# Convolution from high and low parts, and a new order of the last attention turns

## The reference

```
x = x + 0.5 * moe(LN(x))
x = x + attention(LN(x))
x = x + 0.5 * moe(LN(x))

moe(h):       probs = softmax(h @ router.T)            # 8 experts, the best 2, weights normed
              y = sum_k w_k * (silu(h @ gate_k) * (h @ up_k)) @ down_k     # hidden width 176
attention(h): qkv = causal conv over 3 taps, 256 -> 3 * 64, + conv_b
              blocks of 128 tokens; 8 heads of 64 from q, k, v of width 64, causal softmax
              out = (heads @ wo + bo) @ proj_w + proj_b
```

## Time and profile before

| | |
|---|---|
| median of three runs | 769.83 us |
| profiled execution | 768.44 us, of which span 766.7 |
| PE matmul, busy share of the span | 89% |
| DVE | 68% |
| ACT | 64% |
| POOL | 44% |
| PE on the chain that ended last | 66% |
| q/k convolution (L1529) | 192 records, 46.0 us |
| v convolution (L1538) | 192 records, 24.3 us |
| experts' first product (L1474) | 852 records, 288.7 us |
| DMA, first slice of 40 | 308 GB/s |

### The profile page before, as it was taken

The page is one execution under the profiler, slowest core; times in us unless marked ns, Lnnn a source line. Parts: engine busy times, 40 slices in busy tenths (PEclk is TensorE's granted clock), DMA queues, the critical chain, the costliest instruction groups (busy, mean ns, idle before and its releaser), DMA issues.

```text
span 766.7 us, 19140 instructions
## 1 busy us (share of the span) xinstructions
PE 684.0 (89%) x5321; PEld 587.7 (77%) x5354; DVE 519.3 (68%) x1747; ACT 488.2 (64%) x1735; POOL 336.3 (44%) x361
## 2 busy tenths in 40 slices
PE   4999899999997899999999999999418999999854
PEld 3986799999993677777777777777317999999843
DVE  6578666666664666687878787777654777777653
ACT  4767566666663577777777777767514666666533
POOL 5200544444415544446566665444641445444500
PEclk9999999999998999999999999999757999999968
DMA  9940354544432201112121111100243444444289
GB/s 308 316 136 1 95 150 144 144 132 128 125 100 82 71 28 30 32 32 64 57 66 54 64 57 43 41 32 22 90 112 98 122 133 125 131 124 124 84 302 355
DMA packets 57862, 83.39 MB, mean 109 GB/s; under 512 B 9520, under 2 KB 43827, under 8 KB 57780
## 3 DMA queue, kind: packets, MB, share of 16 engines
q1 hardware_dynamic: 44772, 47.63, 19.9%
q0 software_dynamic: 13008, 34.69, 14.6%
HBM read 45.77 MB, written 37.44 MB: 109 GB/s over the span
## 4 chain that ended last, share of the span: by engine, by line
PE 66%; issue 10%; DVE 8%; POOL 7%; DMA 4%; ACT 3%; SPq 1%; DVEq 0%; POOLq 0%; ACTq 0%
PE CC L1474 18%; PE B L1529 3%; PE CC L1557 3%; POOL yg L666 3%; PE A L1461 3%; PE CC L1615 3%; PE SS L1551 3%; PE F L1605 2%; PE SS L1491 2%; POOL pr L658 2%; PE SS L1492 2%; PE SS L1493 2%; PE F L1625 2%; PE SS L1494 2%; PE SS L1495 2%
## 5 line engine op out<-in xcount | busy, mean ns | idle before, releaser
L630 POOL DMA_INDIRECT shared<-h_rows,tok_i x71 | 66.9, 942 | 116.7 <-DVE tok_i L1071 45.1
L642 POOL DMA_INDIRECT y_rows<-shared,y_dest x71 | 69.8, 984 | 89.1 <-DVE y_dest L1139 75.4
L1474 PE MATMUL CC<-w_hi,rowsT_hi 128*128 x284 | 104.6, 368 | 0.3 <-DVE rowsT_lo L1127 0.2
L658 POOL TENSOR_TENSOR pr<-pr,prec 128x1024 f32<-128x1024 f32 x31 | 58.7, 1893 | 94.9 <-DVE prec L1300 94.9
L1474 PE MATMUL CC<-w_hi,rowsT_lo 128*128 x284 | 92.1, 324 | 0.0
L704 ACT ACTIVATE shared<-CC 128x176 f32<-128x176 f32 x142 | 45.1, 317 | 73.9 <-PE CC L1474 73.9
L1474 PE MATMUL CC<-w_lo,rowsT_hi 128*128 x284 | 92.0, 324 | 0.0
L783 ACT ACTIVATE pr<-SS,nmax 128x128 f32<-128x128 f32 x256 | 90.1, 393 | 1.6 <-DVE nmax L1259 1.6
L1122 DVE TENSOR_TENSOR shared<-shared,CC 128x176 f32<-128x176 f32 x142 | 48.0, 338 | 49.9 <-ACT shared L704 47.6
L675 POOL DMA_INDIRECT h_regions<-h_store,dest x64 | 64.0, 1000 | 38.8 <-DVE dest L1224 21.7
L666 POOL DMA_INDIRECT yg<-y_rows,slot_i x64 | 62.3, 973 | 34.4 <-DMA y_rows<-shared 15.5
(11 more groups left out here) (312 smaller groups left out, 2003.2 us busy)
## 6 DMA issues: line engine op xcount, KB each, us to landing
shared<-h_regions SPq DMA_DIRECT2D x71, 129.0 KB
y_rows<-shared SPq DMA_DIRECT2D x71, 128.0 KB, 1.7
w_lo<-y_rows SPq DMA_DIRECT2D x9, 512.0 KB, 8.0
x_sb<-in_x_dram SPq DMA_DIRECT2D x8, 512.0 KB, 7.7
out_dram<-x_sb SPq DMA_DIRECT2D x16, 256.0 KB, 6.3
w_hi<-y_rows SPq DMA_DIRECT2D x7, 512.0 KB, 11.7
w_lo<-in_gupT_dram SPq DMA_DIRECT2D x2, 1408.0 KB, 12.9
h_regions<-pad_rows SPq DMA_DIRECT2D x15, 129.0 KB, 2.8
```

What stands on the lines that cost most here:

```text
L630: pool.indirect_dma_start(out=rows[:, s % RING, 0:D], out_offset=None, in_=h_dram[:, :], in_offset=bass.IndirectOffsetOnAxis(ap=tok_i[:, s ...
L642: pool.indirect_dma_start(out=y_dram[0:TOPK * TOKENS, :], out_offset=bass.IndirectOffsetOnAxis(ap=y_dest[:, s:s + 1], axis=0), in_=y_sb[:, ...
L658: pool.tensor_tensor(pr[:, q, :, :], pr[:, q, :, :], prec[:, q, :].unsqueeze(2).to_broadcast([P, NH, P]), ALU.mult).then_inc(t["norm"], 1)
L1474: i = pe.matmul(CC[:, 512 * (u % 2):512 * (u % 2) + GU], rows_part[:, u % 2, c * P:(c + 1) * P], weights, start=(n == 1), stop=(n == 3 * DC))
```

## The change

Three things are changed together.

1. **The convolution works in float32r from parts.** ACT copies the turned tile into xT_hi; DVE subtracts it from the PSUM tile into xT_lo, in every turn, behind mhaT. In a turn of an odd tile DVE then waits for that result and copies two halos in place of one. PE makes 18 products for q and k (three pairs of parts for each of six), and for v 12 full-width ones: the stationary operand holds high and low part of v's weights side by side, xT_hi and xT_lo pass in turn. The weights' parts are made at the start of attention, three copies on ACT and three subtractions on DVE, and PE waits for them (wprep) before the bias product and `keep_clock`. conv_w is loaded into the tile of tile_oh, after the first layer's token table is read, on SyncE ahead of `store_y`. xT's parts lie where the experts' rowsT and hid parts lie, so DVE waits for the last product of layer one before it clears the halos.
2. **The last turns.** G is no longer rewritten after turn 32; logits of tiles 28 to 31 and the ranks of the late picks get columns of their own, and ACT's copy is 344 columns wide, not 296. Tile 26 and tile 27 are picked singly in turns 32 and 33, tiles 28 and 29 in turn 34, tiles 30 and 31 in turn 36. Comparisons and picks of the late turns are placed differently on DVE, the last projection comes ahead of its turn's logits on PE, and tiles 26 and 27 are sent one by one.
3. **SyncE's row table** (`load_rows`): the first eight registers are loaded before the waits for the sent rows, pads and dummies, not after.

Smaller: the mask is one tile of 128 columns, repeated by a stride of zero; ACT's hT copy waits for xT_lo.

```diff
+        conv_qk = [sb(f"conv_qk_{part}", [P, DC, TAPS * P], F32R) for part in ("hi", "lo")]
+        conv_v = sb("conv_v", [P, DC, TAPS, 2 * W], F32R)
...
-        PICKS = {9: (0, 4), 13: (4, 4), 17: (8, 4), 21: (12, 4), 25: (16, 4), 29: (20, 4), 31: (24, 2), 32: (26, 2),
-                 35: (28, 2), 36: (30, 2)}
+        PICKS = {9: (0, 4), 13: (4, 4), 17: (8, 4), 21: (12, 4), 25: (16, 4), 29: (20, 4), 31: (24, 2), 32: (26, 1),
+                 33: (27, 1), 34: (28, 2), 36: (30, 2)}
+        LAST_WRITE = TILES
+        LAST_LG = LAST_WRITE - POST
+        RANKS_AT = {27: D + E, 28: D + 2 * E, 30: LG_AT + (TILES - LAST_LG) * E}
...
                 for first in range(0, TABLE_TILES, 8):
+                    if first == 0:
+                        sp.wait_ge(T["row_table"], 1)
                     sp.load(regs, row_i[0:1, first:first + 8])
+                    if first == 0:
+                        for q in range(GROUP):
+                            sp.wait_ge(T[f"sent{q}"], 32 * TILES // GROUP)
...
+            sp.wait_ge(loaded, 16 * len(loads))
+            sp.wait_ge(first["tokens"], 1)
+            sp.dma_start(conv_sb, conv_w).then_inc(loaded, 16)
             store_y(0)
...
+                a.activation(conv_qk[0][:, :, :], conv_sb_qk, ACT.Copy).then_inc(wprep, 1)
+                for c in range(DC):
+                    a.activation(conv_v_parts[0][:, c, :, :], conv_sb_v[:, c, :, :], ACT.Copy).then_inc(wprep, 1)
...
-                    if i > 0:
+                    if 0 < i <= LAST_WRITE:
...
-                    if there(i + 3) and (i + 3) % 2:
+                    if there(i + 3):
...
+                        v.wait_ge(t["xT_hi"], b + 1)
+                        ins = v.tensor_tensor(xT_lo[:, p % 2, :, at_b:at_b + P],
+                                              A[:, 0:D].rearrange("p (c n) -> p c n", c=DC),
+                                              xT_hi[:, p % 2, :, at_b:at_b + P].bitcast(F32), ALU.subtract)
+                        if b % 2:
+                            step(ins)
+                            after(v, t["conv"], 2 * p)
+                            for part in (xT_hi, xT_lo):
...
+                v.wait_ge(wprep, 7 + 1 + DC)
+                v.tensor_tensor(conv_qk[1][:, :, :], conv_sb_qk, conv_qk[0][:, :, :].bitcast(F32), ALU.subtract
+                                ).then_inc(wprep, 1)
...
+                        for c, k in taps:
+                            for n, (weights, part) in enumerate(CONV_PARTS):
+                                x = pe.matmul(B[:, 0:2 * P], weights[:, c, k * P:(k + 1) * P],
+                                              part[:, p % 2, c, k:k + 2 * P], start=((c, k) == taps[0] and n == 0),
+                                              stop=((c, k) == taps[-1] and n == 2), skip_group_check=True)
...
+                    if i - 2 == TILES - 1:
+                        project(i - 2)
+                        pe.wait_ge(t["res"], TILES)
...
+            pe.wait_ge(wprep, 7 + 2 * (1 + DC))
             pe.matmul(G[:, 0:D], ones_r[:, :], projb_parts[:, :], start=True, stop=True).then_inc(projb, 1)
             keep_clock(F[:, :], 44)
```

More of the change, by code:

```diff
@@ L1513, in keep_clock, with project @@
                 for _ in range(n):
-                    pe.matmul(bank, ident_bf[:, :], mask_bf[:, :], start=True, stop=True, skip_group_check=True)
+                    pe.matmul(bank, ident_bf[:, :], mask_4, start=True, stop=True, skip_group_check=True)
             def attention():
                 t = T
+                CONV_PARTS = (conv_qk[0], xT_hi), (conv_qk[1], xT_hi), (conv_qk[0], xT_lo)
+                taps = [(c, k) for c in range(DC) for k in range(TAPS)]
+                def project(b):
+                    pe.wait_ge(t["mhaT"], b + 1)
+                    pe.matmul(G[:, 0:D], mhaT[:, :], proj_sb[:, :], start=False, stop=True, skip_group_check=True
+                              ).then_inc(t["out"], 1)
                 def turn(i):
@@ L1561, in turn @@
                         pe.wait_ge(t["normed"], b + 1)
[L1562 removed]
+                        after(pe, t["xT_lo"], b)
                         after(pe, t["hT"], i - POST + 1)
@@ L1589, in turn @@
                         x.then_inc(t["logits"], 1)
-                    if there(i - 2):
-                        pe.wait_ge(t["mhaT"], i - 1)
-                        if there(i - 1 - POST):
-                            pe.wait_ge(t["lg"], i - POST)
-                        pe.matmul(G[:, 0:D], mhaT[:, :], proj_sb[:, :], start=False, stop=True,
-                                  skip_group_check=True).then_inc(t["out"], 1)
+                    if there(i - 2) and i - 2 < TILES - 1:
+                        project(i - 2)
                     if there(i - 1):
```

146 lines of the change are left out of this document (79 added, 67 removed).

## The result

The changed kernel takes 777.31 us in the median of four runs (776.00 to 777.90), the kernel before 770.02 (769.14 to 770.52) beside it: a ratio of 1.0097, 95% interval 1.0080 to 1.0113. Run again later, on another chip, it was 777.89 against 768.85, ratio 1.0107 (1.0085 to 1.0130). The change costs about 8 us; 778.0 was predicted. The profiled execution took 777.9 us, 776.2 of it span.

The account below looks back on a forecast made before the run. DVE was taken to bound the pick stretches (22 of every 36.5 us), PE just behind: 768.4 + 4.9 + 5.5 + 0.5 - 2.7 = 776.6, plus 1.4 to the median, 778.0 us; eight-in-ten range 765 to 783.

Parts of the forecast that it names:

- The start: Start of attention: keep-clock products wait for split weights, run partly at half clock and delay the first convolution, +4.9 us.
- DVE's term: Attention turns: DVE's added low parts cost +1.3 us a cycle, +6.6 over five cycles, +5.5 in all.
- The step on which the forecast turned: Pick turns: PE's vo product already waits for DVE's mhaT, so what PE saves is paid for on DVE.
- the sign: Pick turns: L1625's wait growing from 0.28 to above 1 us would show the forecast right.
- the even turn: DVE in odd-tile turns: subtraction, wait for its own result and second halo copy add 0.64 us.
- the row's 0.22: DVE's wait for its own result, from profile strides of 0.56 us with it against 0.34 without.
- The convolution's gain: q/k convolution on PE: 18 products in 2.16 us, 0.43 less a pair, 6.9 for 16 pairs; lost in waits.
- PE is the bound: Rival for the turns: PE bounds them, gaining 6.5 us, but the start costs 4.9; 766.0 us, chance 0.12.
- Layer one: Layer one's first gather: loading conv_w shares the rings and delays the first rows, +0.5 us.
- The tail: Last turns: earlier picks and sends and SyncE's earlier row table save 2.7 us, between -1.5 and -4.
- From the profiled run to the median: Final step of the sum: the median lies 1.4 us above the profiled run, as in the kernel before.

Follow-up runs that it names:

- late_wait: The changed kernel with PE's wait for the split weights moved behind the 44 keep-clock products: 774.86 us, ratio 1.0080 to the kernel before.

## Why the prediction was right, point by point

- **The start, +4.9 predicted, +5.1 found.** Right in size and in its two causes' places: weights ready at 235 (234.8 predicted), products at half clock, first transposes behind them, the second tile's low part by 252.4 (251.7). Up to the first convolution's start the queue costs 4.1 us (22.24 less 18.13 in late_wait) and DVE's later low part of the second tile 1.5 (18.13 less 16.62); the convolution itself, quicker at half clock too, gives back 0.5. The distances differ by 0.9 us between profiles of the early wait (21.9 to 22.8), so the parts are good to about that.
- **DVE's term, +5.5 predicted, +4.9 found.** The step on which the forecast turned holds: the gated vo product. Its wait in pick turns is 1.19 to 1.24 us in five of five, above the 1 us named as the sign. Of its terms the subtraction was exact (0.33 for 0.34); the even turn was 0.60 and not 0.64, as the stride of 0.56 had been taken from the residual and its statistics, a pair with a costlier wait. The Trainium skill's rule cited there ("VectorE: DVE Perf Modes", section "The DRAIN you can't avoid": a semaphore after each operation costs nothing extra) and the row's 0.22 miss the 0.11 us found by as much: it isn't nothing, and only half of the row. Four of the five cycles grew by 1.1 to 1.5 us where 1.3 was forecast, but the last, from turn 25 to 29, by 0.5: together 5.6 and not 6.6. Before turn 9 the changed kernel gained 0.7 (0.8 forecast) and from turn 29 on 0.5 (0.3 forecast). The rest, 0.5 the other way, is where the stage begins, behind a first convolution that is quicker. The place was incomplete: the working had transposes late in one even turn, and the trace has three waits of 0.3 to 0.5 us in a cycle. And one term of DVE's is missing: its operation `at` stands 0.78 us in the turn without a pick where it stood 0.45 before, behind POOL's scaling (rows in the last section). No run shows what that costs the cycle.
- **The convolution's gain.** 0.45 us a pair on PE, as costed. That it would be lost in pick turns and after them was right (1.4 of 6.5 us kept). The rival "PE is the bound" gave 6.5 us for the case in which DVE hides all; with DVE's work taken out altogether, 4.2 came. That rival was priced too low in time, since DVE gates pick turns already before the change.
- **Layer one, +0.5 predicted, +0.67 found.** Right by chance. The gather's delay of 0.8 us is real, but the first gather also started earlier in the changed kernel (77.43 in its first profile, 78.0 to 78.5 in later ones, against 78.95), so that PE's first rows came at 81.00 and not later than before (81.75). The rest goes with the clock (0.83 for 1.00 between 80 and 90 us).
- **The tail, -2.7 predicted, -1.4 found.** The term was mis-sized, just outside its own range (-1.5 to -4). Measured from the last v convolution, the places of tiles 28 and 29 came 2.4 us earlier than in the earlier trace rows (567.51) and those of 30 and 31 0.7 earlier (573.49), much as worked out (2.4 and 1.1). The working then followed POOL's sends and gave the pads 1.1 us; it said that they share the DMA engines but not that they would land last. In the chain they do, 5.24 us after the last one's start, and splitting their issue gives the end back to the sends, which then need 6.05. Following one queue to its end is not enough when another writes through the same engines.
- **From the profiled run to the median, +1.4 predicted.** The median was 0.6 us below the profiled run, not above. The terms of the sum missed the profiled run by 1.3 us, nearly all of it the tail, and this step by 2.0 the other way, so that 778.0 came closer to 777.3 than its parts deserve.

## What to carry over

Work taken from a nearly bound engine and paid for on its partner is worth only what both together let through: fill in the table of two by two (light and loaded, quick and slow) before adding up gains, since here 4.2 and 6.3 us gave neither their difference nor their sum. Where an engine's warm-up stands in a queue, place the new wait behind it and not ahead. And of a change in three parts time each alone: the tail alone makes the kernel before 0.3% quicker, while the convolution hides that gain.

## What the runs showed of the hardware

- A DVE operation on 128 x 4 elements with both inputs in SBUF stood up to 1.45 us while POOL multiplied SBUF tiles for 1.89 us, and took 0.15 when POOL did not. The Trainium skill has this ("SBUF — State Buffer", section "Who interferes with whom": a DVE instruction with two SBUF inputs contends with a GpSimd instruction that reads SBUF, the shared ports are an exclusive lock, and the order of issue decides who blocks), and the trace agrees. The changed kernel's halo copies, like those before, lie where POOL does not compute, and stay at 0.24 us for two. But its `at`, two columns, does not. Before, then in the changed kernel, it ends with POOL's scaling (424.33 and 433.90):

```profile
423.89 0.45 DVE L1246 SCALAR_TENSOR_TENSOR at<-arstd 128x2 f32<-128x2 f32 x1
```

```profile
432.01 1.89 POOL L683 TENSOR_TENSOR pr<-pr,prec 128x1024 f32<-128x1024 f32 x1 [1.23 <-DVE prec L1340]
433.14 0.78 DVE L1273 SCALAR_TENSOR_TENSOR at<-arstd 128x2 f32<-128x2 f32 x1 [0.29 <-ACT arstd L775]
```

- 44 products of 512 columns did not keep the clock for a convolution that started 5 us after them: the granted clock was 1.00 (2.4 GHz) in 248 to 250, 0.52 in the next window and 0.50 (1.2 GHz) in 252 to 254. Nor did it matter whether there were 44 or 22: with 22 it was 0.50 from 248 to 252, with the convolution from 249.01.
- The clock can differ in the same ten microseconds between runs of kernels that are the same up to there (1.00, 0.83 or 0.66 between 80 and 90 us), and layer one's end differs with it by up to 3 us. For differences below 0.5% the stages of a profile were a better measure than six runs.
- On two chips DVE stood mostly near 2 us at a time, 13 to 16 times a run, released by nothing the profile names; the kernel before took 40 us more there, though it was not profiled on them. What it is stays open.
